# Gate logits with tokens as rows, a route in two parts, and routing masks by comparison, in a perceiver block with mixture of experts

## The chip, the cores and the metric

The kernel runs on one core of a Trainium2 chip. A core has TensorE (matrix products into PSUM banks), VectorE, ScalarE and GpSimd for element-wise work, and SyncE, whose queue issues most DMAs. The engines run their own instruction streams and meet at semaphores. The metric is the device time of one execution in microseconds (us), as the median of three runs. Names in the profile: PE is TensorE, PEld its weight loads, DVE is VectorE, ACT is ScalarE, POOL is GpSimd, SP is SyncE.

## The reference

A block on `x` of 2 batches x 512 tokens x 512 features, with a context of 2 x 8192 x 512. Three residual layers, all in float32:

```python
x = x + cross_attention(layernorm(x), ctx)      # five linear maps, softmax over 8192 keys
x = x + ssm(layernorm(x))                       # state space layer as a long convolution by FFT, gated by silu
x = x + ffn(layernorm(x))                       # mixture of experts

def ffn(x):                                     # 8 experts, one per token
    xt = x.reshape(-1, 512)                     # 1024 tokens
    gates = softmax(xt @ gate_w + gate_b)       # gate_w: 512 x 8
    sel = argmax(gates, axis=-1)                # the first of equal ones
    onehot = one_hot(sel, 8)
    y_all = einsum('td,edh->eth', xt, expert_w) + expert_b[:, None, :]
    return einsum('te,eth->th', onehot, y_all)
```

The change concerns only the last layer: how the expert of each token is found, and how the tokens are gathered for the experts.

## The kernel before

The attention over both batches takes the first 930 us or so. The rest, the tail, is: the gated convolution (spectra, products of spectra on VectorE, back to time, gate), the output projection, then the expert layer. Everything is ordered by hand: each engine has one function `tail()` that calls its steps in the order in which they stand in the queue, and a step waits on semaphores that count finished jobs. `JOBS` lists all results that TensorE leaves in a PSUM bank, in its order; bank numbers follow from the position in that list, modulo 8, and a bank is opened once what stood in it before has been read.

Float32 products at high precision are made in three passes over a high part (rounded, "hi") and a low part (the rest, "lo") of each operand. ScalarE rounds the high parts; the low parts are made by GpSimd or VectorE. `gated_lo` on GpSimd (L2164) makes those of batch 0's gated output, `gated_lo` on VectorE (L1813) those of batch 1, `lo_tiles` (L2020) those of the first four experts' weights W0 to W3, `weight_los` (L1947, VectorE) those of all others.

The expert layer, step by step:
- `turn_ffn` (L974, TensorE): turns the 8 token tiles (128 tokens x 512 features) of the sum `xb`; ScalarE copies each from its bank into `spectra` (`turned_ffn`, L1320). In ScalarE's queue that stands behind `weights(3)`, the rounding of W3, which waits for the load of W3.
- `gate_logits` (L981): products of `gate_raw` (stationary, 128 features x 8 experts) with the turned tokens (moving, 512 or 256 tokens), so that a logit is found at (expert, token). ScalarE copies 8 rows per batch to SBUF (`copy_logits`), and `turn_logits` (L992) turns them by eight small transposes to (token, expert).
- `gate` (L1862, VectorE): completes the layer norm of the logits, finds the largest, and the one-hot `hits`.
- `rank_tokens` (L1001, TensorE): products with the masks `before` (1 where column > partition) and `ones`, which give each token's rank within its expert, and the number of tokens per expert.
- `route` (L1901, VectorE): 15 groups of 128 slots are filled. Groups 0 to 7 hold the first 128 tokens of each expert; a token of rank 128 or more goes to one of 7 spare groups. From rank and counts it finds `lane` (the slot in the group) and `group`, and builds `place` (128x1024, 1 where the token's lane is the column) and `numbered` (token number where the token's group is the column).
- `place_tokens` (L1012, TensorE): 8 products of `place` with `numbered` give, for each slot of each group, the token's number. VectorE makes integer row numbers of them (L1932 for the gather, L1934 for the scatter).
- `gather` (L2199, GpSimd): an indirect DMA fetches the normalized tokens and the sum for the 128 rows of a group from the DRAM tensor `mixed`. It waits also for the stores of both into `mixed` (`store_x`, `store_rows` on SP) and for W3's low parts.
- `turn_tokens` and `mix` (L1020, L1029, TensorE): turn a group's tokens, and 12 products with the group's expert and one with the bias. ScalarE rounds the turned tokens, VectorE makes the low part (`turned_lo`, L1954), then adds the result to the sum (`add_mixed`), and GpSimd scatters the rows to the output.
- `split_expert_bias` (L1891, VectorE): four operations that make high and low parts of the experts' bias, needed by the last product of mix.0.

SP issues in this order (L599 to L620): W0; bias; W1; W2; W4; `store_x(0)`; W3; W5; `store_x(1)`; four `store_rows`; W6; W7; then the seven chosen experts. W3, like W0, goes to the buffer `stage[0]` and waits for W0's low parts as well.

On GpSimd the order is: low parts of the convolution's output; routing numbers (`lanes`, which holds 0 to 127 along a row, among them); the output bias into batch 0's residual; `gated_lo`; `routing_masks` (L2187), which waits until VectorE's products of spectra are done, since it uses their scratch row `obB`; the output bias into batch 1's residual (`add_out_bias(1)`, L2156); W0 to W3.

## Time and profile before

| | us |
|---|---|
| median of 3 runs | 1134.09 |
| lowest, highest | 1133.72, 1135.25 |
| the profiled execution | 1134.54 |
| its span in the trace | 1132.8 |
| busy in the span: TensorE | 1093.9 |
| VectorE | 841.3 |
| ScalarE | 530.5 |
| GpSimd | 537.5 |
| mean granted clock of TensorE | 0.985 of full speed |

TensorE is busy for 97% of the span. Times in the trace are from the span's start. A row of the timeline gives start, duration, engine, line, operation, output and inputs, and how many instructions were merged; the brackets at its end hold the idle time of the engine before the row, and what ended it. The granted clock is 1.00 at full speed (2.4 GHz) and 0.50 at the lower level (1.2 GHz). Matrix products of float32 that aren't split show two passes each, so that four of them are eight instructions in a row of the trace.

### The profile page before, as it was taken

Reading aid. Unit: us, or ns where it says so; the run is one execution under the profiler, and the core shown is the slowest. Engines: PE = TensorE matmul, PEld = TensorE weight load, DVE = VectorE, ACT = ScalarE, POOL = GpSimd, SP = SyncE. Lnnn points to the kernel's source line nnn. Section 1 sums busy time; section 2 is a strip of 40 time slices with the busy share of each in tenths; the row PEclk is TensorE's granted clock in tenths of the full one; section 3 lists DMA queues with packets and bytes.
Section 4 is the critical chain, followed back from the end, with each engine's and each line's share of the span. In section 5 each row is a group of like instructions: output and inputs, shape, how many; then the busy total and the mean of one; then the engine's idle time right before and its main releaser. Section 6 shows DMA issues by size and latency. Waiting matters only on the chain.

```text
span 1132.8 us, 16497 instructions
## 1 busy us (share of the span) xinstructions
PE 1093.9 (97%) x4969; PEld 884.5 (78%) x4969; DVE 841.3 (74%) x1756; ACT 530.5 (47%) x1127; POOL 537.5 (47%) x588
## 2 busy tenths in 40 slices
PE   7999999999999999999999999999999999998498
PEld 5787877878888888888888888888888888886375
DVE  6963498799888888778357777776777657699584
ACT  4221056556555555533464444444444444356462
POOL 3700445345444544411266666665765632177253
PEclk8999999999999999999999999999999999999699
DMA  8211368977876787432429767766876541025991
GB/s 292 84 53 59 52 153 211 218 194 190 204 179 185 190 192 195 140 87 99 76 73 203 193 187 202 187 191 171 213 185 177 179 161 38 1 76 161 323 398 66
DMA packets 199351, 182.26 MB, mean 161 GB/s; under 512 B 17873, under 2 KB 144881, under 8 KB 199299
## 3 DMA queue, kind: packets, MB, share of 16 engines
q1 hardware_dynamic: 178658, 140.21, 48.3%
q10 hardware_dynamic: 17280, 31.46, 7.9%
q0 software_dynamic: 3360, 9.97, 2.4%
q8 instruction: 24, 0.39, 0.1%
q14 instruction: 29, 0.23, 0.1%
HBM read 141.73 MB, written 41.68 MB: 162 GB/s over the span
## 4 chain that ended last, share of the span: by engine, by line
PE 80%; DVE 8%; POOL 4%; DMA 3%; issue 3%; SPq 1%; ACT 1%; POOLq 0%; ACTq 0%; DVEq 0%
PE bank L644 39%; PE bank L783 28%; PE bank L1040 4%; PE bank L837 3%; PE bank L652 1%; PE bank L1026 1%; DMA stage<-in_L_xattn_hW_dram 1%; DVE h L1527 1%; DMA stage<-in_L_ffn_expert_w_dram 1%; DMA spectra<-in_ctx_dram 1%; PE bank L987 1%; PE bank L678 1%; POOL hl_C L2023 1%; PE bank L1045 1%; POOL hl_B L2039 1%
## 5 line engine op out<-in xcount | busy, mean ns | idle before, releaser
L1187 ACT ACTIVATE probs<-bank,nbias 128x512 f32<-128x512 f32 x128 | 88.1, 688 | 242.3 <-DVE nbias L1650 242.1
L783 PE MATMUL bank<-hl_F,probsT 128*128 128x512 f32 x768 | 190.4, 397 | 0.6 <-issue 0.4
L783 PE MATMUL bank<-hl_A,probsT 128*128 128x512 f32 x768 | 190.4, 396 | 0.0
L644 PE MATMUL bank<-hl_B,hl_D 128*128 128x512 f32 x768 | 185.7, 391 | 1.8 <-POOL hl_B L2039 1.4
L1645 DVE TENSOR_REDUCE mx<-bank 128x1 f32<-128x512 f32 x128 | 88.0, 687 | 133.9 <-PE bank L644 133.9
L644 PE MATMUL bank<-hl_C,hl_D 128*128 128x512 f32 x768 | 185.3, 390 | 0.0
L783 PEld LDWEIGHTS bank<-hl_F,probsT 128*128 128x128 f32 x768 | 144.1, 188 | 35.4 <-issue 0.8
L783 PEld LDWEIGHTS bank<-hl_A,probsT 128*128 128x128 f32 x768 | 144.1, 188 | 34.3 <-POOL hl_A L2032 0.2
L644 PEld LDWEIGHTS bank<-hl_B,hl_D 128*128 128x128 f32 x768 | 143.7, 188 | 34.1 <-issue 2.3
L644 PEld LDWEIGHTS bank<-hl_C,hl_D 128*128 128x128 f32 x768 | 144.1, 188 | 31.7 <-issue 0.3
L2032 POOL TENSOR_TENSOR hl_F<-stage,hl_F 128x512 fp32r<-128x512 f32 x64 | 84.7, 1323 | 162.2 <-ACT hl_F L1152 162.1
L2032 POOL TENSOR_TENSOR hl_A<-stage,hl_A 128x512 fp32r<-128x512 f32 x64 | 84.2, 1315 | 145.4 <-ACT hl_A L1152 145.4
L1691 DVE SCALAR_TENSOR_TENSOR rows<-rows,alpha,bank 128x512 f32<-128x512 f32 x128 | 90.9, 710 | 14.9 <-PE bank L783 14.9
L1662 DVE TENSOR_TENSOR probsT<-bank,probsT 128x512 fp32r<-128x512 f32 x128 | 87.3, 682 | 1.9 <-ACT probsT L1174 1.8
L1174 ACT ACTIVATE probsT<-bank 128x512 fp32r<-128x512 f32 x128 | 74.2, 580 | 10.8 <-PE bank L770 10.7
L1152 ACT ACTIVATE hl_F<-stage 128x512 fp32r<-128x512 f32 x64 | 40.4, 632 | 27.7 <-issue 18.2
L1152 ACT ACTIVATE hl_A<-stage 128x512 fp32r<-128x512 f32 x64 | 40.4, 632 | 27.6 <-issue 18.3
L2039 POOL TENSOR_TENSOR hl_C<-spectra,hl_C 128x512 fp32r<-128x512 f32 x32 | 40.9, 1292 | 22.9 <-ACT hl_C L1160 22.9
L2039 POOL TENSOR_TENSOR hl_C<-xb,hl_C 128x512 fp32r<-128x512 f32 x32 | 41.0, 1292 | 20.2 <-ACT hl_C L1160 20.2
L1667 DVE STREAM_TRANSPOSE bank<-resid 128x512 f32<-128x512 f32 x60 | 43.0, 716 | 9.4 <-DMA resid<-p_rows 9.4
L1683 DVE SCALAR_TENSOR_TENSOR lsum<-lsum,alpha,rsum 128x1 f32<-128x1 f32 x128 | 49.0, 383 | 0.0
L1699 DVE SCALAR_TENSOR_TENSOR zT<-h,cbdt,zT 128x512 f32<-128x512 f32 x64 | 46.6, 728 | 0.0
(419 smaller groups left out, 1862.6 us busy)
## 6 DMA issues: line engine op xcount, KB each, us to landing
p_rows<-probs ACTq DMA_DIRECT2D x120, 256.0 KB, 3.1
stage<-in_ctx_dram SPq DMA_DIRECT2D x112, 256.0 KB, 3.2
spectra<-in_ctx_dram SPq DMA_DIRECT2D x64, 256.0 KB, 5.9
xb<-in_ctx_dram SPq DMA_DIRECT2D x64, 256.0 KB, 5.9
resid<-p_rows SPq DMA_DIRECT2D x240, 64.0 KB, 2.1
h<-p_rows SPq DMA_DIRECT2D x120, 64.0 KB, 2.5
obB<-p_rows SPq DMA_DIRECT2D x120, 64.0 KB, 2.0
stage<-in_L_ffn_expert_w_dram SPq DMA_DIRECT2D x6, 1024.0 KB, 6.9
```

The lines of the kernel that those rows point to most:

```text
L644: last = nc.tensor.matmul(dst, lhs[:, a, t, k * P:(k + 1) * P], rhs[:, c, t, :], start=(t == 0 and (a, c) == PASSES[0]), stop=(t == T - 1 ...
L783: last = nc.tensor.matmul(obank[u % 2][:], probsT[u % 2][:, a, j, :], nat[b][par][:, c, j, :], start=(j == 0 and (a, c) == PASSES[0]), sto ...
L1152: nc.scalar.activation(nat[b][par][:, 0, j, :], stage[par][:, j, :], ACT.Copy).then_inc(nat_hi, 1)
L1174: nc.scalar.activation(dst, src, ACT.Copy).then_inc(pT_hi, 1)
L1187: nc.scalar.activation(dst, src, ACT.Exp, bias=nbias[:, q:q + 1], scale=SCALE, accum_out=rsum[:, q:q + 1]).then_inc(probs_ready, 1)
L1645: nc.vector.tensor_reduce(mx[:, col], sbank[u % 2][:], AX_X, ALU.max).then_inc(stat_done, 1)
L1662: nc.vector.tensor_tensor(lo, src, hi, ALU.subtract).then_inc(pT_split, 1)
L1683: nc.vector.scalar_tensor_tensor(lsum[:, col], lsum[:, col], alpha[:, u:u + 1], rsum[:, col], ALU.mult, ALU.add).then_inc(sums_updated, 1)
L1691: nc.vector.scalar_tensor_tensor(rows[:, q, :], rows[:, q, :], alpha[:, u:u + 1], obank[u % 2][:], ALU.mult, ALU.add).then_inc(rows_added, 1)
L1699: nc.vector.scalar_tensor_tensor(kern[:, k, :], h[u % 2][:], weight, kern[:, k, :], ALU.mult, ALU.add).then_inc(term_added, 1)
L2032: nc.gpsimd.tensor_tensor(nat[b][par][:, 1, j, :], stage[par][:, j, :], nat[b][par][:, 0, j, :].bitcast(F32), ALU.subtract).then_inc(nat_s ...
L2039: nc.gpsimd.tensor_tensor(by_squares(ctxT[par][:, 1])[:, dd], square(squares[b][par], dd), by_squares(ctxT[par][:, 0])[:, dd].bitcast(F32) ...
```

## The change

Six edits:
1. Logits by tokens. `gate_logits(n)` now takes the turned tile as the stationary operand and `gate_raw` as the moving one: four products of 128x128 with 128x8 per tile, which leave the logits at (token, expert) in the bank `logit_columns` at once. The jobs `logits@0`, `logits@1`, `copy_logits` and `turn_logits` go. The products of a tile follow two turned tiles behind.
2. Route in two parts. Groups 0 to 7 need only the rank and the token's own expert, so a first `place` is built from `rank`, and `slots.0` gives gather and scatter rows for them. The rest of the route follows, and a second `place` from `lane` and `slots.1` for the spare groups.
3. The second turn of tokens is put into mix.0, behind its first three products.
4. Masks by comparison: `ones` is `lanes` x 0 + 1, `before` is `lanes` > `partition`; no scratch, so no wait for the products. They stand before `gated_lo`.
5. W0's low parts stand right behind `gated_lo`, now with the wait for the products in front of them, and `add_out_bias(1)` behind them.
6. `split_expert_bias` stands behind the route instead of before `gate`.

```diff
@@ JOBS @@
-             + tiles_at(0, "x_ssm")[2:] + tiles_at(1, "x_ssm") + tiles_at(0, "ffnT") + tiles_at(1, "ffnT")[:2]
-             + ["logits@0"] + tiles_at(1, "ffnT")[2:] + ["logits@1", "logit_columns", "ranks", "slots"] + MIX_JOBS)
+             + tiles_at(0, "x_ssm")[2:] + tiles_at(1, "x_ssm") + tiles_at(0, "ffnT") + tiles_at(1, "ffnT")
+             + ["logit_columns", "ranks"] + (["slots.0", "slots.1"]) + MIX_JOBS)
@@ TensorE @@
-                for t in range(T):
-                    turn_ffn(0, t)
-                for t in range(2):
-                    turn_ffn(1, t)
-                gate_logits(0, 1)
-                for t in range(2, T):
-                    turn_ffn(1, t)
-                gate_logits(1, 2)
-                turn_logits()
+                for n in range(B * T + 2):
+                    if n < B * T:
+                        turn_ffn(n // T, n % T)
+                    if n >= 2:
+                        gate_logits(n - 2)
                 rank_tokens()
-                place_tokens()
+                place_tokens("slots.0", 1, 0, E)
+                place_tokens("slots.1", 2, E, E)
                 turn_tokens(0)
                 for g in range(GROUPS):
-                    if g + 1 < GROUPS:
+                    if 0 < g < GROUPS - 1:
                         turn_tokens(g + 1)
                     mix(g)
...
+            def gate_logits(n):
+
+                dst = bank_of("logit_columns")
+                if n == 0:
+                    open_bank("logit_columns")
+                evacuated_from(f"ffnT.{n % T}@{n // T}")
+                for k in range(T):
+                    last = nc.tensor.matmul(dst[:, n * E:(n + 1) * E], spectra[:, n, k * P:(k + 1) * P], gate_raw[:, k, :],
+                                            start=(k == 0), stop=(k == T - 1))
+                if n == B * T - 1:
+                    last.then_inc(filled, 1)
...
+            def place_tokens(job, count, first, width):
+
+                pe.wait_ge(ranked, count)
+                dst = open_bank(job)
                 for n in range(B * T):
-                    last = nc.tensor.matmul(dst[:, 0:2 * E], place[:, n, :], numbered[:, n, :], start=(n == 0), stop=(n == B * T - 1))
+                    last = nc.tensor.matmul(dst[:, 0:width], place[:, n, :], numbered[:, n, first:first + width],
+                                            start=(n == 0), stop=(n == B * T - 1))
...
@@ mix, in the loop over t @@
+                    if g == 0 and t == 0:
+                        turn_tokens(1)
@@ ScalarE @@
                 turned_ffn(0, range(T))
-                turned_ffn(1, range(2))
-                copy_logits(0)
-                turned_ffn(1, range(2, T))
-                copy_logits(1)
+                turned_ffn(1, range(T))
@@ VectorE, gate @@
                 dve.wait_ge(iota_made, 1)
+                nc.vector.tensor_tensor(numbered[:, :, 0:E], hits.bitcast(F32), of_token(token), ALU.mult)
@@ VectorE, route @@
-                nc.vector.tensor_reduce(rank, hit_value, AX_X, ALU.add)
+                link(nc.vector.tensor_reduce(rank, hit_value, AX_X, ALU.add))
+                place_at(rank)
...
+                filled_by(dve, "slots.0")
+                nc.vector.tensor_scalar(gather_rows[:, 0:E], bank_of("slots.0")[:, 0:E], float(FAR), float(TOKENS - 1),
+                                        ALU.add, ALU.min).then_inc(indexed, 1)
...
+                place_at(lane)
+                choose_experts()
+                filled_by(dve, "slots.1")
+                nc.vector.tensor_scalar(gather_rows[:, E:GROUPS], bank_of("slots.1")[:, 0:SPARE], float(FAR), float(TOKENS - 1),
+                                        ALU.add, ALU.min).then_inc(indexed, 1)
...
+            def place_at(m):
+
+                nc.vector.tensor_tensor(place, m.unsqueeze(2).to_broadcast([P, B * T, P]),
                                         lanes.unsqueeze(1).to_broadcast([P, B * T, P]), ALU.is_equal).then_inc(ranked, 1)
@@ VectorE, tail @@
                 scale_outputs()
-                split_expert_bias()
                 gate()
                 route()
+                split_expert_bias()
@@ GpSimd, routing_masks @@
-                pool.wait_ge(product_step, PRODUCTS * (TRIPS + 2))
-                whole = obB[:, 2 * P:3 * P]
-                chain(nc.gpsimd.memset(whole, 1.0))
-                nc.gpsimd.tensor_copy(ones, whole).then_inc(table_made, 1)
-                pool.wait_ge(table_made, 1)
-                chain(nc.gpsimd.affine_select(out=whole, in_=whole, compare_op=ALU.is_gt, fill=0.0, base=0,
-                                              pattern=[[1, P]], channel_multiplier=-1))
-                nc.gpsimd.tensor_copy(before, whole).then_inc(table_made, 1)
+                pool.wait_ge(iota_made, 1)
+                nc.gpsimd.tensor_scalar(ones, lanes, 0.0, 1.0, ALU.mult, ALU.add).then_inc(table_made, 1)
+                nc.gpsimd.tensor_scalar(before, lanes, partition, None, ALU.is_gt).then_inc(table_made, 1)
@@ GpSimd, tail @@
                 add_out_bias(0)
+                routing_masks()
                 gated_lo()
-                routing_masks()
+                pool.wait_ge(product_step, PRODUCTS * (TRIPS + 2))
+                lo_tiles("W0", raw[BUF["W0"]], weights_hl[0])
                 add_out_bias(1)
-                for g in range(EARLY):
+                for g in range(1, EARLY):
                     lo_tiles(f"W{g}", raw[BUF[f"W{g}"]], weights_hl[g])
...
                 for g in range(ROWS_KEPT):
                     gather(g)
+                pool.wait_ge(indexed, 2)
```

The order of instructions on TensorE around the logits, before: `ident,xb` are the turns of a tile, `spectra,gate_raw` the logits, `ident,probs` the first of the small transposes.

```order
L978 MATMUL bank<-ident,xb 128x128 [waits evacuated]
L978 MATMUL bank<-ident,xb 128x128 x3
L987 MATMUL bank<-spectra,gate_raw 8x512 [waits copied,evacuated]
L987 MATMUL bank<-spectra,gate_raw 8x512 x3
L978 MATMUL bank<-ident,xb 128x128 [waits evacuated]
L978 MATMUL bank<-ident,xb 128x128 x3
```

And after the change, where the pattern repeats for every tile:

```order
L974 MATMUL bank<-ident,xb 128x128 [waits evacuated]
L974 MATMUL bank<-ident,xb 128x128 x3
L984 MATMUL bank<-gate_raw,spectra 128x8 [waits copied]
L984 MATMUL bank<-gate_raw,spectra 128x8 x3
L974 MATMUL bank<-ident,xb 128x128 [waits evacuated]
L974 MATMUL bank<-ident,xb 128x128 x3
L984 MATMUL bank<-gate_raw,spectra 128x8 [waits copied]
```

The wide products, four for a batch, became four narrow ones for each tile; each group of four waits for the copy of its own tile alone.

VectorE from the rank on, after the change: `place` is written by L1927 (twice), the gather rows by L1901 and L1921, the bias split is L1880 to L1883, and L1951 is the low part of the first turned tokens.

```order
L1927 TENSOR_TENSOR dft<-ssm_in,ssm_w 128x1024 [waits link_done]
L1896 TENSOR_TENSOR ssm_in<-ssm_in,ssm_w 128x56
L1898 TENSOR_REDUCE ssm_in<-ssm_in 128x8 [waits link_done]
L1899 SCALAR_TENSOR_TENSOR ssm_in<-ssm_w,ssm_in 128x8 [waits link_done]
L1901 TENSOR_SCALAR gather_rows<-bank 128x8 [waits filled,link_done]
...
L1921 TENSOR_SCALAR gather_rows<-bank 128x7 [waits filled]
L1923 TENSOR_SCALAR scatter_rows<-bank 128x7
L1880 CAST dft<-probs 16x512 [waits iota_made,in_eb]
L1881 TENSOR_TENSOR h<-probs,dft 16x512 [waits link_done]
L1882 SCALAR_TENSOR_TENSOR probs<-h,ssm_w 16x512 [waits link_done]
L1883 SCALAR_TENSOR_TENSOR dft<-dft,ssm_w,probs 16x512 [waits link_done]
L1951 TENSOR_TENSOR probsT<-bank,probsT 128x512 [waits rounded]
```

Before, these four operations of the bias stood ahead of `gate`, there was one `place` (L1928) near the end of the route, and L1957, the low part of the first turned tokens, followed the scatter rows directly.

GpSimd in the tail, before: L2192 to L2197 are the masks, `zT<-zT,h` the output bias into batch 1's residual, `hl_C<-stage` W0's low parts, `hl_F<-zT` the gated low parts.

```order
L2167 TENSOR_TENSOR hl_F<-zT,hl_F 128x512 [waits gated_hi0] x4
L2192 MEMSET obB 128x128 [waits product_step,filled]
L2193 CAST dft<-obB 128x128 [waits table_step]
L2195 AFFINE_SELECT obB<-obB 128x128 [waits table_made]
L2197 CAST dft<-obB 128x128 [waits table_step]
L2162 TENSOR_TENSOR zT<-zT,h 128x512 [waits resid_scaled,in_outb]
L2162 TENSOR_TENSOR zT<-zT,h 128x512 [waits resid_scaled] x3
L2023 TENSOR_TENSOR hl_C<-stage,hl_C 128x512 [waits split_hi] x4
```

And after:

```order
L2185 TENSOR_SCALAR dft<-ssm_w 128x128 [waits iota_made,filled]
L2186 TENSOR_SCALAR dft<-ssm_w 128x128
L2161 TENSOR_TENSOR hl_F<-zT,hl_F 128x512 [waits gated_hi0] x4
L2017 TENSOR_TENSOR hl_C<-stage,hl_C 128x512 [waits split_hi,product_step]
L2017 TENSOR_TENSOR hl_C<-stage,hl_C 128x512 [waits split_hi] x3
L2156 TENSOR_TENSOR zT<-zT,h 128x512 [waits resid_scaled,in_outb]
L2156 TENSOR_TENSOR zT<-zT,h 128x512 [waits resid_scaled] x3
```

The masks moved ahead of the gated low parts, and W0's low parts ahead of the bias into batch 1's residual.

## Rows read from the trace of the kernel before

**Rows 1.** Timeline of TensorE: start and duration in us, then the row

```profile
1034.63 2.78 PE L978 MATMUL bank<-ident,xb 128*128 128x128 f32 x24
1040.23 3.59 PE L987 MATMUL bank<-spectra,gate_raw 128*8 128x512 f32 x8 [2.82 <-ACT spectra L1224]
...
1051.67 0.30 PE L1007 MATMUL bank<-onehot,dft 128*128 128x64 f32 x1 [2.19 <-DVE onehot L1885]
...
1058.46 1.88 PE L1017 MATMUL bank<-dft 128*128 128x16 f32 x8 [4.86 <-DVE dft L1928]
1066.20 1.09 PE L1026 MATMUL bank<-ident,spectra 128*128 128x128 f32 x4 [5.86 <-DMA spectra<-mixed,gather_rows]
1068.95 1.09 PE L1026 MATMUL bank<-ident,spectra 128*128 128x128 f32 x4 [1.67 <-DMA spectra<-mixed,gather_rows]
1069.69 4.28 PE L1040 MATMUL bank<-hl_C,probsT 128*128 128x512 f32 x12
...
1074.74 3.06 PE L1040 MATMUL bank<-hl_B,probsT 128*128 128x512 f32 x12
```

**Rows 2.** Timeline of ScalarE, same columns

```profile
1035.95 2.19 ACT L1341 ACTIVATE hl_F<-stage 128x512 fp32r<-128x512 f32 x4 [3.54 <-DMA stage<-in_L_ffn_expert_w_dram]
1038.05 3.00 ACT L1224 ACTIVATE spectra<-bank 128x512 f32<-128x512 f32 x6
...
1048.93 2.91 ACT L1330 ACTIVATE rows<-xb,ffn_shift,rstd 128x512 f32<-128x512 f32 x4
```

**Rows 3.** Timeline of SyncE's queue, same columns

```profile
1027.72 0.37 SPq L554 DMA_DIRECT2D mixed<-xb  x1
1028.13 0.51 SPq L437 DMA_DIRECT2D stage<-in_L_ffn_expert_w_dram  x1
```

**Rows 4.** Timeline of GpSimd, same columns

```profile
994.20 11.85 POOL L2167 TENSOR_TENSOR hl_F<-zT,hl_F 128x512 fp32r<-128x512 f32 x4 [27.39 <-ACT hl_F L1288]
...
1010.00 2.16 POOL L2193 CAST dft<-obB 128x128 fp32r<-128x128 f32 x1
...
1017.85 6.85 POOL L2023 TENSOR_TENSOR hl_C<-stage,hl_C 128x512 fp32r<-128x512 f32 x4
```

**Rows 5.** Timeline of VectorE, same columns

```profile
1001.54 1.67 DVE L376 TENSOR_TENSOR spectra<-probs,obB 128x512 f32<-128x512 f32 x1
...
1043.76 0.41 DVE L1895 CAST dft<-probs 16x512 fp32r<-16x512 f32 x1
...
1045.69 0.74 DVE L1898 SCALAR_TENSOR_TENSOR dft<-dft,ssm_w,probs 16x512 fp32r<-16x512 f32 x1
...
1049.59 0.23 DVE L1876 TENSOR_TENSOR logit<-bank,ssm_in 128x64 f32<-128x64 f32 x1 [3.02 <-PE bank L998]
...
1054.10 0.22 DVE L1909 TENSOR_REDUCE ssm_in<-ssm_in 128x8 f32<-128x64 f32 x1
...
1054.72 0.22 DVE L1913 TENSOR_TENSOR ssm_in<-ssm_in,ssm_w 128x56 f32<-128x56 f32 x1
...
1057.19 1.22 DVE L1928 TENSOR_TENSOR dft<-ssm_in,ssm_w 128x1024 fp32r<-128x1024 f32 x1
...
1060.37 0.17 DVE L1932 TENSOR_SCALAR gather_rows<-bank 128x15 int32<-128x15 f32 x1 [1.06 <-PE bank L1017]
...
1067.95 0.69 DVE L1957 TENSOR_TENSOR probsT<-bank,probsT 128x512 fp32r<-128x512 f32 x1 [7.32 <-ACT probsT L1347]
1068.56 2.49 DVE L1951 TENSOR_TENSOR hl_E<-stage,hl_E 128x512 fp32r<-128x512 f32 x4
```

**Rows 6.** Line L897: duration min/median/max in ns, first and last start

```profile
L897 PE MATMUL bank<-gate_raw,one x8: 256/256/276, 938.8 to 939.6; 128*128 128x8 f32 x8
```

**Rows 7.** Gathers into `qc`, line L2202, same columns

```profile
L2202 POOL DMA_INDIRECT qc<-mixed,gather_rows x3: 933/1382/1414, 1069.2 to 1107.0; - x3
```

**Rows 8.** Two stretches: length, TensorE's busy time, clock, DMA share, GB/s

```profile
932.00:940.00 8.00, 7.94 (x58) 1.00 0.26 101
1066.00:1073.00 7.00, 5.14 (x17) 0.54 0.98 335
```

53 lines of the change are left out of this document (12 added, 41 removed).

## Prediction

> **What bounds the kernel now.** I read the slices, then the chain of waits over the last 100 us, then each engine's timeline from 990 us. The attention stages are bound by TensorE and the change doesn't touch them. It touches the stretch from about 994 us to the first expert product (mix.0) at 1069. Behind that, TensorE runs 15 experts back to back, so the last instruction moves as mix.0 moves. The question is therefore: when do the first turned tokens and mix.0 start?
>
> In that stretch TensorE waits six times [rows 1]: 2.82 us for copied turned tiles (until 1040.23), then for the logits to come through a copy, 2.19 us for the one-hot, 4.86 us for VectorE's route (until 1058.46), 5.86 us for the first gather (until 1066.20), 1.67 us for the second (until 1068.95). Three orders stand behind these waits:
> - ScalarE copies turned tiles only after W3's split, which waits 3.54 us for W3 to land and ends at 1038.1 [rows 2]. SP issues W3 at 1028.13, right behind the store of batch 0 at 1027.72 [rows 3]. It is a queue behind VectorE's last sum of batch 0. The chain of waits blames GpSimd's splits, but W0's split ended at 1017.85 + 6.85 = 1024.7 [rows 4], 3.4 us before.
> - VectorE works on the route from 1053.7 to 1058.4 [rows 5], TensorE then forms the slots in 1.88 us [rows 1], and gather rows follow at 1060.37.
> - mix.0 stands behind the second gather on TensorE.
>
> **Logits by tokens.** Removed: the wide products (3.59 us, and as much again for batch 1), two copies of 8 rows and eight small transposes behind them. Added: 8 tiles x 4 products, stationary 128x128, moving 8 columns. The same form stands in L897: its 8 passes (two per product) start between 938.8 and 939.6, so one each 0.115 us [rows 6]. A tile costs 4 x 2 x 0.115 = 0.92 us, eight cost 7.3 us. Their advantage is the start: the first needs one copied tile, not four. Copies run at 3.00 / 6 = 0.5 us spacing from 1038.05, the first is done at 1038.65 [rows 2], and TensorE starts about 1038.8. Only three of eight tiles are turned by then, five remain at 2.78 / 6 = 0.46 us [rows 1]. End: 1038.8 + 7.3 + 5 x 0.46 + about 0.1 = 1048.5 to 1048.7. VectorE got its logits at 1049.59. The gain is 0.9 us; bounds 0 (each tile pays its fill of 0.1 to 0.15) and 1.6 (switching between tiles hides some loads, start at once).
>
> ScalarE loses the two copies and so normalizes earlier than 1048.93, by about 2.5 us; row stores and the loads of W6 and W7 go earlier with it. Hidden, but needed: the gather waits for those stores. They now stand ready at about 1056, the gather rows at 1056.8: 0.7 us of cover. Uncovered it costs up to 1 us.
>
> **Route in two parts.** Before: hits x ranks, rank (L1909, 1054.10 + 0.22), 15 small operations, and place until 1057.19 + 1.22 = 1058.41 [rows 5]. Now place (1.22) stands right behind rank: 1054.35 to 1055.57. TensorE's slots.0 takes 1.88 again (its loads set it, not 8 or 16 columns): 1057.50. The gather rows of the eight fixed experts are at 1057.5 instead of 1060.37, 2.9 us earlier. The three small operations between hide under TensorE. But the second part begins only then: from L1913 to the end of place it was 1058.41 - 1054.72 = 3.69 us, which gives about 1061.3. TensorE has slots.1 in its queue ahead of the first turned tokens, so it is busy with that until 1061.3 + 1.9 = 1063.2. The first gather, at its old distance 1066.20 - 1060.37 = 5.83, lands at 1063.3: the two meet, and slots.1 costs nothing so far.
>
> **The bias split behind the route.** It was hidden in VectorE's wait for logits: 1043.76 to 1045.69 + 0.74 = 1046.43, 2.67 us [rows 5]. Now it follows scatter rows.1 and stands ahead of the turned tokens' low part: 1063.4 to 1066.0. The turned tokens would be ready for it at 1063.3 + 1.75 = 1065.0 (1067.95 - 1066.20 before), so it costs 1.0 us. The low part (0.69) ends at 1066.7 and mix.0 starts at about 1066.75.
>
> **Mixing one before the second turn.** Before, TensorE's unbroken work began with the second turn at 1068.95. Now it begins with mix.0's first three products, and the second turn sits inside; the work is the same. So the gain counts from 1068.95 to 1066.75: 2.2 us. With the 0.9 of the logits: 3.1 us. Bounds of this part: 1.2 (gather 1 us later, because more of W6 and W7 is in flight) to 3.2 (the bias split hidden entirely).
>
> **Masks and W0 on GpSimd.** The masks lose a memset, a select and their wait. They move from 1010 into the 27.39 us in which GpSimd was idle before 994.20 [rows 4]; ScalarE's order (spectra copied before the gated tiles that release 994.20) puts them there. Two tensor_scalar of 128x128 are new; the nearest row, a cast of that size, took 2.16 us while VectorE worked on two SBUF inputs, and one of 512 columns free of that costs about a quarter of 5 us. So 0.3 us each on their own. But they fall in VectorE's product stretch. There GpSimd's four low parts took 11.85 us, and a VectorE operation of 0.6 took 1.67 us [rows 4, 5]. Each mask can hold VectorE once for its own length, or wait itself and push the low parts. VectorE is what leads to the store at 1027.72, to W3 and the logits, one for one. Bounds 0 and 1.5 us (two masks, each holding a product and the low parts behind them); I take 0.6.
> W0's split now runs from 1010 on, and the out bias follows. SP issues W3 behind the store anyway, so this brings nothing; the out bias is needed after 1027 and ends by 1024. Which of GpSimd's tiles meets VectorE's gated low parts changes: plus or minus 0.5, taken as 0. The scatters' wait for indexed 2 (1063.4) is over long before mix.0 ends.
>
> **A rule against it.** VectorE's second part and the bias split now run beside GpSimd's gathers; before, GpSimd stood idle during the route. The rows that show such a pair: hl_E's low parts took 2.49 us for four, undisturbed [rows 5], and the gathers into qc, of which the first started beside them, took 0.93 us at least and 1.41 at most [rows 7], so GpSimd gave way. The linked small operations leave gaps, and there it could be the other way. I take 0.2 us.
> The Trainium skill, "SBUF — State Buffer" (section on the two sides and the shared port pair), says that VectorE with two SBUF inputs and GpSimd hold the pair exclusively, the loser waiting a whole instruction. By that rule a gather could stop the linked chain again and again. The trace agrees for GpSimd's tensor_tensor (1.67 instead of 0.6 us) and, for gathers, only in that they lengthen.
>
> **Sum.** 0.9 + 2.2 - 0.6 - 0.2 = 2.3 us. The profiled run took 1134.54 us (span 1132.8 and 1.7 around it), 0.45 above the median 1134.09; 2.3 off each gives 1132.2 and 1131.8. The forecast is 1131.8.
>
> **Rivals.**
> 1. The clock returns earlier (chance 0.12). It was low as mix.0 began: 1066 to 1073 has a mean of 0.54 [rows 8], which is 0.50 until about 1072.4 and 1.00 from there. Now slots.1 and the first turn stand against each other, and work goes on sooner, so mix.0 could run at full clock: 3.06 instead of 4.28 us [rows 1], and the turn at half its 1.09: up to 1.6 us more, 1130.2. Against it: it took 3.4 us of unbroken work from 1068.95, and the turn at 1066.20 had not raised it.
> 2. The gain is eaten upstream (0.24): masks cost 1.5 in place of 0.6, or the row stores become the gather's last wait (1 us), or logits bring nothing. Gain about 1.0: 1133.1.
> 3. Slower, by the ports (0.07). Gathers stop VectorE in the second part and the bias split. Two or three gathers fall in the former and two in the latter, at 0.93 us each: up to 4.65 us, of which 0.2 is counted. The change loses from the third such stop on; at five it is 4.45 - 2.3 = 2.15 us later than before: 1136.2. For it: linked operations leave gaps. Against: the gathers gave way where both ran.
> 4. Slower, by the clock (0.05). TensorE now does only turns and 8-column products from 1034.6 to 1048.6. If it falls to the low level around 1042, the remaining 6.6 us double: 1138.4. Against it: from 932 to 940 TensorE did turns and L897's products only and stayed at 1.00 [rows 8].
> 5. Nothing moves (0.02): something else orders the first gather.
>
> **Numbers.** The forecast has 0.50. About 0.2% (2.27 us) is what can be told from no change. The forecast lies on that edge. Half of its cases and all of rival 1 and a little of rival 2 count as faster: 0.52; slower by more 0.08; the rest 0.40. The forecast's own range is 1130.8 to 1132.8; with rivals 1 and 2 and the bounds above, 1129.9 to 1134.2, which leaves out rivals 3 and 4 and a little at the low end.
>
> **What would show it.** Right: the first 8-column product near 1038.8 to 1039.5, logits taken at 1048.7, gather rows about 3.7 us earlier than 1060.37, slots.1 ending as the first gather lands, the bias split right ahead of the first low part, mix.0 near 1066 (all plus what the masks cost). Wrong: a second product tile spacing above 1.0 us; a clock below 1.00 before 1049; small VectorE operations of 1 us in the second part; GpSimd's first gather released by a store and not by the gather rows; W3 issued apart from the store of batch 0.

## The result, and the profile after

| | before | after |
|---|---|---|
| median of 20 runs, us | 1135.66 | 1139.28 |
| lowest, highest | 1133.15, 1138.63 | 1135.82, 1143.66 |
| profiled run and its span | 1134.54, 1132.8 | 1137.05, 1135.0 |

The ratio is 1.0031, 95% interval 1.0022 to 1.0041: the change makes the kernel 3.5 us slower, where 2.3 us faster was forecast. The sign is wrong, and the time lies outside the range.

The changed kernel's TensorE timeline (start and duration in us, then the row; a bracket is the idle time ahead and what ended it), for [rows 1]:

```profile
1035.64 1.47 PE L974 MATMUL bank<-ident,xb 128*128 128x128 f32 x12
1038.15 1.03 PE L984 MATMUL bank<-gate_raw,spectra 128*128 128x8 f32 x8 [1.03 <-ACT spectra L1215]
1039.03 0.64 PE L974 MATMUL bank<-ident,xb 128*128 128x128 f32 x4
1039.50 0.96 PE L984 MATMUL bank<-gate_raw,spectra 128*128 128x8 f32 x8
1040.32 0.63 PE L974 MATMUL bank<-ident,xb 128*128 128x128 f32 x4
1040.79 1.67 PE L984 MATMUL bank<-gate_raw,spectra 128*128 128x8 f32 x8
...
1048.10 5.13 PE L984 MATMUL bank<-gate_raw,spectra 128*128 128x8 f32 x24
1055.42 0.42 PE L995 MATMUL bank<-onehot,dft 128*128 128x64 f32 x1 [2.19 <-DVE onehot L1869]
...
1059.58 1.87 PE L1005 MATMUL bank<-dft 128*128 128x8 f32 x8 [2.03 <-DVE dft L1927]
1065.34 1.87 PE L1005 MATMUL bank<-dft 128*128 128x8 f32 x8 [3.89 <-DVE dft L1927]
1067.32 1.09 PE L1015 MATMUL bank<-ident,spectra 128*128 128x128 f32 x4
1070.82 1.62 PE L1029 MATMUL bank<-hl_C,probsT 128*128 128x512 f32 x3 [2.41 <-DVE probsT L1951]
...
1072.94 3.26 PE L1029 MATMUL bank<-hl_C,probsT 128*128 128x512 f32 x9
```

The first two tiles of gate products take 1.03 and 0.96 us, the third 1.67, and all others 1.71 or 1.72 (the last row is three of them in 5.13). The turns go from 0.64 to 1.09. The granted clock goes with it; stretches of TensorE with length, then the busy time of TensorE, of its weight loads, VectorE, ScalarE and GpSimd, then clock, DMA share and GB/s. The first and the last row answer [rows 8]:

```profile
932.00:940.00 8.00, 8.00 (x48) 6.17 (x46) 5.91 (x10) 5.48 (x12) 6.85 (x16) 1.00 0.01 2
1034.00:1040.00 6.00, 4.97 (x38) 4.40 (x37) 5.69 (x14) 3.94 (x8) 3.96 (x4) 1.00 0.10 37
1040.00:1046.00 6.00, 6.00 (x36) 6.00 (x35) 2.99 (x13) 1.60 (x4) 1.00 (x1) 0.57 0.49 139
1046.00:1052.00 6.00, 6.00 (x30) 6.00 (x30) 0.00 (x0) 4.14 (x7) 0.00 (x0) 0.50 0.69 258
...
1066.00:1073.00 7.00, 4.48 (x18) 3.65 (x18) 6.05 (x14) 0.60 (x1) 5.48 (x6) 0.50 0.91 293
```

The clock falls from 2.4 to 1.2 GHz at about 1041 and stays there, though TensorE is busy for all of 1040 to 1052. It is at 0.50 in mix.0 as well: its last nine products take 3.26 us.

The other engines. ScalarE, SyncE's queue, GpSimd and VectorE, for [rows 2 to 5]:

```profile
1035.33 2.19 ACT L1328 ACTIVATE hl_F<-stage 128x512 fp32r<-128x512 f32 x4 [3.42 <-DMA stage<-in_L_ffn_expert_w_dram]
1037.43 1.55 ACT L1215 ACTIVATE spectra<-bank 128x512 f32<-128x512 f32 x3
...
1048.84 2.91 ACT L1317 ACTIVATE rows<-xb,ffn_shift,rstd 128x512 f32<-128x512 f32 x4
```

```profile
1027.22 0.37 SPq L553 DMA_DIRECT2D mixed<-xb  x1
...
1053.19 1.77 SPq L559 DMA_DIRECT2D mixed<-zT  x2
```

```profile
1006.31 6.71 POOL L2017 TENSOR_TENSOR hl_C<-stage,hl_C 128x512 fp32r<-128x512 f32 x4 [3.64 <-DVE spectra L375]
...
1062.66 1.24 POOL L2191 DMA_INDIRECT spectra<-mixed,gather_rows  x1 [21.66 <-DVE gather_rows L1901]
```

```profile
1006.15 2.38 DVE L1794 TENSOR_TENSOR hl_D<-spectra,hl_D 128x512 fp32r<-128x512 f32 x2
1008.46 3.42 DVE L1794 TENSOR_TENSOR hl_B<-spectra,hl_B 128x512 fp32r<-128x512 f32 x2
...
1053.34 0.23 DVE L1860 TENSOR_TENSOR logit<-bank,ssm_in 128x64 f32<-128x64 f32 x1 [9.97 <-PE bank L984]
...
1061.56 0.17 DVE L1901 TENSOR_SCALAR gather_rows<-bank 128x8 int32<-128x8 f32 x1 [1.45 <-PE bank L1005]
...
1067.25 0.17 DVE L1921 TENSOR_SCALAR gather_rows<-bank 128x7 int32<-128x7 f32 x1 [0.81 <-PE bank L1005]
1067.40 0.41 DVE L1880 CAST dft<-probs 16x512 fp32r<-16x512 f32 x1
...
1070.00 0.67 DVE L1951 TENSOR_TENSOR probsT<-bank,probsT 128x512 fp32r<-128x512 f32 x1
```

VectorE gets its logits at 1053.34, not at 1048.7. It waited 9.97 us for them. The gather is released by the gather rows, as forecast. ScalarE starts to normalize at 1048.84, 0.1 us earlier than before and not 2.5: it copies the turned tiles first, and they came late too. VectorE's low parts of batch 1's convolution output (L1794, L1810 before) were 1.28 us for two before; they took 2.38 and 3.42 beside GpSimd's W0, which now starts in the same stretch.

The lines that answer to [rows 6, 7], with durations (min/median/max) in ns and first and last start:

```profile
L896 PE MATMUL bank<-gate_raw,one x8: 256/256/276, 935.3 to 936.1; 128*128 128x8 f32 x8
```

```profile
L2191 POOL DMA_INDIRECT qc<-mixed,gather_rows x3: 938/1152/2152, 1071.7 to 1110.7; - x3
```

To compare executions, I cut each timeline at four places: the first turn of `turn_ffn`; the first product released by the one-hot; the first product of mix.1; the end of the span. Each number is a difference of starts in that kernel's TensorE timeline.

| us | first turn at | to one-hot | to mix.1 | to end | span |
|---|---|---|---|---|---|
| before | 1034.63 | 17.04 | 23.07 | 58.06 | 1132.8 |
| after | 1035.64 | 19.78 | 21.55 | 58.03 | 1135.0 |
| after, second execution (e12) | 1034.98 | 24.22 | 22.43 | 58.07 | 1139.7 |

So the loss is in the logits (2.7 and 7.2 us), the route gives back 1.5 and 0.6, and behind mix.1 nothing has changed. The two executions differ in the logits because in e12 the first gate product starts 4.61 us behind the first turn (2.51 in the first), and its first tile already takes 1.74 us: the clock went down as it began. The row of before is one of the better executions of that kernel as well: in e2, e4, e7 and e8, whose logits are as before, the one-hot comes 18.70 to 19.28 us behind the first turn and not 17.04 (why is shown under e9).

### The profile page after: what moved, and what is told of

The parts are those of the page before. It is cut to its first block, busy times and chain, and to the rows that moved or that the text cites. A ratio compares the mean times of both kernels' runs of the same rounds, so it can differ in the third digit from the quotient of the medians.

```text
span 1135.0 us, 16577 instructions
## 1 busy us (share of the span) xinstructions
PE 1100.4 (97%) x5009; PEld 896.1 (79%) x5009; DVE 844.2 (74%) x1760; ACT 530.3 (47%) x1125; POOL 538.9 (47%) x586
## 3 DMA queue, kind: packets, MB, share of 16 engines
q0 software_dynamic: 3360, 9.97, 2.5%
## 4 chain that ended last, share of the span: by engine, by line
PE 83%; DVE 11%; DMA 2%; issue 1%; SPq 1%; ACT 1%; POOL 1%; POOLq 0%; ACTq 0%; DVEq 0%
PE bank L643 40%; PE bank L782 30%; PE bank L1029 4%; PE bank L836 2%; PE bank L651 1%; PE bank L984 1%; DVE probs L375 1%; PE bank L1015 1%; DVE h L1511 1%; DMA stage<-in_L_ffn_expert_w_dram 1%; DMA spectra<-in_ctx_dram 1%; DVE spectra L375 1%; PE bank L1036 1%; PE bank L677 1%; DVE bnst L1489 0%
```

## The experiments

**Which edit loses the time.** Three kernels, each the kernel before with one edit or one group.

`e3_logits_alone`: before with edit 1 alone.

```diff
...
-    gate_logits(0, 1)
...
-    gate_logits(1, 2)
-    turn_logits()
+    for n in range(B * T + 2):
+        if n < B * T: turn_ffn(n // T, n % T)
+        if n >= 2: gate_logits(n - 2)
...
```

> The kernel before with the logits by tokens alone. Theory B: the clock falls to 0.50 within the logits, they are ready about 3.5 to 4.5 us later than before, and the kernel is that much slower. Rival C: no gap ahead of it, so the clock stays at 1.00, the logits are ready 0.9 us earlier and the kernel is 0.9 us faster.

Measured: 1139.75 us against 1134.2, ratio 1.0044 (1.0030 to 1.0058), +5.0 us. In its TensorE timeline one-hot comes 22.66 us after the first turn, 5.6 later than before, and mix.1 follows 23.12 after that, as before.

```profile
1039.02 1.03 PE L983 MATMUL bank<-gate_raw,spectra 128*128 128x8 f32 x8 [2.83 <-ACT spectra L1211]
1039.91 0.64 PE L973 MATMUL bank<-ident,xb 128*128 128x128 f32 x4
1040.38 1.58 PE L983 MATMUL bank<-gate_raw,spectra 128*128 128x8 f32 x8
...
1050.06 5.13 PE L983 MATMUL bank<-gate_raw,spectra 128*128 128x8 f32 x24
```

By themselves the narrow logits cost as much as the whole change or more (+3.4 to +6.6 us against +2.5 to +4.7, by the intervals). The first half of the expectation came true, with 5.0 us where 3.5 to 4.5 were expected.

`e2_gpsimd_alone`: before with edits 4 and 5 (masks by comparison and early, W0 behind the gated lows).

```diff
-    gated_lo()
-    routing_masks()
+    routing_masks()
+    gated_lo()
+    pool.wait_ge(product_step, PRODUCTS * (TRIPS + 2))
+    lo_tiles("W0", raw[BUF["W0"]], weights_hl[0])
...
```

> The kernel before with the GpSimd edits alone (masks by comparison and early, W0's low parts right behind the gated ones). Theory A: VectorE's four low parts take 5 to 6 us, TensorE waits about 3.5 us for them, the kernel is 2.5 to 3 us slower than before. Rival D: the early masks cost it, in VectorE's product stretch; then VectorE's products there are over 1 us longer and the four low parts as before.

Measured: 1134.51 us, ratio 0.9997 (0.9984 to 1.0010). GpSimd's new order can't be told from no change (-1.8 to +1.1 us). VectorE's L1810 takes 1.28 us twice there, so neither of the two cases that were expected came true.

`e4_route_alone`: before with edits 2, 3 and 6.

```diff
-    place_tokens()
+    place_tokens("slots.0", 1, 0, E)
+    place_tokens("slots.1", 2, E, E)
...
-    split_expert_bias(); gate(); route()
+    gate(); route(); split_expert_bias()
...
```

> The kernel before with the route in two parts, the bias split behind it and the second turn inside mix.0. Both theories: the part of the forecast that held, 1.9 to 2.2 us faster than before; slots.1 and the bias split lie between the first gather and mix.0. Rival E (ports in the route): small VectorE operations beside the gathers stretch, and it is under 1 us faster.

Measured: 1135.48 us, ratio 1.0011 (0.9996 to 1.0026): no gain, where 1.9 to 2.2 us were expected. One-hot to mix.1 is 23.69 us, against 23.07 before. Its GpSimd and TensorE timelines:

```profile
1057.61 1.25 POOL L2216 DMA_INDIRECT spectra<-mixed,gather_rows  x1 [18.99 <-DMA mixed<-zT]
```

```profile
1065.26 1.09 PE L1028 MATMUL bank<-ident,spectra 128*128 128x128 f32 x4 [4.02 <-DMA spectra<-mixed,gather_rows]
```

Its gather rows are written at 1055.59, but the gather starts only at 1057.61, 2.02 us later where it is 1.10 before (1060.37 to 1061.47), and what releases it is a row store. It then needs 7.65 us until TensorE can turn its rows; before it was 1066.20 - 1061.47 = 4.73 (turn from [rows 1], gather from this row of before):

```profile
1061.47 1.25 POOL L2202 DMA_INDIRECT spectra<-mixed,gather_rows  x1 [19.87 <-DVE gather_rows L1932]
```

**Is GpSimd's W0 part of the loss?** VectorE's slow low parts (L1794) in the first profile suggested so.

`e1_w0_behind_lows`: after, with GpSimd's W0 low parts held until those of VectorE (L1794) are done.

```diff
-    pool.wait_ge(product_step, PRODUCTS * (TRIPS + 2))
+    pool.wait_ge(y_lo_done[1], 2 * T)
```

> The changed kernel, but GpSimd starts W0's low parts only when VectorE's four last low parts of batch 1's output are done, not when the products are. Theory A (ports): W0's low parts stretched those four from 2.5 to 5.8 us and made TensorE wait 3.46 us; here they take 2.5 us again, TensorE waits less than 0.6 us there, and the kernel is 2.8 us faster than the changed one, at +0.8 us against before. Theory B (clock): the products of 8 columns let the clock fall in the logits by themselves; it falls here too, near the third tile. Rival C: the clock fell in the logits only as a late effect of that 3.46 us gap; then it stays at 1.00 here, and the kernel is 6 to 7 us faster than the changed one, 3 us faster than before.

Measured: 1138.9 us, ratio 1.0046 (1.0028 to 1.0065). L1794 is 1.28 twice there, and the time is no better than after's. The first theory, that this was most of the loss, failed, and so did rival C: the clock falls in the logits without that stop of TensorE. Theory B came true; here the fall is within the second tile.

`e12_after_again`: the changed kernel once more.

> The changed kernel again, to see in a second execution what varies from run to run. Expected: 1139 us, granted clock 0.981 over the span, the gate products at 1.71 us each from 1041 on. Of the stop of VectorE in the evacuation of the lows (L1794: 2.38 and 3.42 us in the first profile, 1.28 twice in the kernels without it) one theory says it belongs to the changed order and comes back with the same durations; the other says it is a race between GpSimd's product and VectorE's evacuation that is lost only in some executions: 1.28 twice here, with no change of the median.

Measured: 1138.89 us, ratio 1.0037 (1.0023 to 1.0051). VectorE's timeline of the unchanged order:

```profile
1009.60 1.28 DVE L1794 TENSOR_TENSOR hl_D<-spectra,hl_D 128x512 fp32r<-128x512 f32 x2
1010.81 1.28 DVE L1794 TENSOR_TENSOR hl_B<-spectra,hl_B 128x512 fp32r<-128x512 f32 x2
```

GpSimd's W0 begins at 1009.76 there, behind VectorE's 1009.60. In the first profile it was 1006.31 behind 1006.15: the same 0.16 us, and another outcome. So it varies from execution to execution: of the five profiles with W0 in this place, two show 2.38 and 3.42 or near it (after and e14) and three 1.28 twice (e2, e12, e13). The first profile lost 4.5 us there (TensorE waited 3.46 us for `hl_B`, then three of its groups behind ran at the low clock). How often it happens isn't known; e1, in which it can't, has the same median as e12. In its span it hardly shows, because that execution was early: the products of [rows 6] started at 938.8 before and at 935.3 after, 3.5 us ahead in code that the change doesn't touch, and the first turn 1.0 us behind.

**Why the clock falls.** In e1, e3 and e12 it falls within 1.5 us of the end of a gap of 2.65 to 3.13 us, so their traces can't separate two theories (in after the gap is 1.03 us, and the clock falls 2.7 us behind it): there are no wide products in the stage any more (they would hold or restore the clock); or it is the gap of TensorE ahead of the stage that lowers it.

`e5_logits_one_wide` and `e6_logits_three_wide`: e3 with one, or three, unused products of 448 columns ahead of each tile's gate products.

```diff
     evacuated_from(f"ffnT.{n % T}@{n // T}")
+    for _ in range(1):    # 3 in e6
+        nc.tensor.matmul(dst[:, 64:512], probsT_all[:, 0, 0, 0, :], inverse[...], start=True, stop=True)
     for k in range(T):
```

> The kernel before with logits by tokens, and one extra product of 448 columns (0.19 us, result unused, into columns of the same bank that nothing reads) ahead of each tile's four. Theory B (clock, because the stage has no wide products): the clock stays at 1.00 through the logits or comes back within them; the four products of a tile take about 1.0 us, the logits are ready 1 to 3 us earlier than with logits by tokens alone, although 1.5 us of work is added. Rival F (the clock falls there whatever TensorE does, or one wide product per tile is too little): as with logits by tokens alone or 1.5 to 3 us slower than that.

> The same with three extra wide products per tile (0.57 us each tile, 4.5 us in all at full clock). Theory B: clock 1.00 from the third tile on at the latest, each tile's own products 1.0 us, logits ready at about the same time as with logits by tokens alone (4.5 us more work, 4.5 us less by the clock). Rival F: the clock stays at 0.50, and the logits come 4.5 to 9 us later than with logits by tokens alone.

Measured: 1145.16 us, ratio 1.0077 (1.0050 to 1.0104), and 1152.37 us, ratio 1.0150 (1.0120 to 1.0180). Both are slower than expected (one-hot 4.9 and 11.4 us later behind the first turn than in e3; at most 3 and 9 were expected). TensorE stood 3.37 and 3.97 us ahead of the first extra product, and the clock was at 0.50 from that product on (0.71 us for it in e5), every gate tile took 1.71, and it never returned. One to three wide products among the narrow ones don't bring the clock back. Whether they could have held it isn't tested, since it was down before they began.

`e9_fill_before_logits`: before (wide logits) with 11 unused products of 512 columns in TensorE's gap ahead of the first logits product.

```diff
     dst = open_bank(f"logits@{b}")
+    if b == 0:
+        filler(dst, 11)    # matmul(dst, probsT_all[...], inverse[...][:, 0:512])
...
```

> The kernel before with nothing changed but 11 products of 512 columns, whose result nobody reads, put into TensorE's gap of some 2.8 us between its last work of stage one and the first logits product (a bf16 pass of that width at full clock is about 0.21 us, so they just fill the gap). Theory A: what drops the granted clock at the logits is the idle stretch just ahead of them; then the first eight wide logits products (L987 there) take 3.6 us and not the 5.28 us that four of my earlier profiles with wide logits show, the window over the logits reads 1.00, and the kernel is about 1.7 us faster than before's median run. Rival B: the fall is due to the turns and the light work over the last 10 us, and the fillers move nothing: 5.28 us again, ratio 1.000. Rival C: the fillers run at half clock themselves and push the logits back by up to 2 us: 1.5 us slower.

Measured: 1133.52 us against 1135.18, ratio 0.9984 (0.9972 to 0.9997), -1.8 us. The first of the two rows is e2's, the second e9's; both are the first eight wide products:

```profile
1040.49 5.28 PE L987 MATMUL bank<-spectra,gate_raw 128*8 128x512 f32 x8 [2.79 <-ACT spectra L1224]
```

```profile
1038.36 3.60 PE L996 MATMUL bank<-spectra,gate_raw 128*8 128x512 f32 x8 [0.33 <-ACT spectra L1233]
```

The kernel before loses its clock at the logits too, in some executions. Of six profiles with wide logits and the gap, four show 5.28 or 5.29 us (e2, e4, e7, e8) and two 3.59 (before and e13); all four with the gap filled show 3.60. But with wide products it comes back inside the stage. e2's stretches:

```profile
1040.00:1046.00 6.00, 5.51 (x11) 1.14 (x12) 5.48 (x17) 1.52 (x4) 1.87 (x2) 0.72 0.36 106
1046.00:1052.00 6.00, 5.09 (x32) 2.55 (x30) 1.26 (x4) 3.10 (x6) 0.00 (x0) 1.00 0.68 243
```

`e10_narrow_with_fill`: e3 with 10 such products ahead of the first gate product.

```diff
     if n == 0:
         open_bank("logit_columns")
+        filler(dst, 10)
```

> The kernel before with the logits by tokens alone (as e3_logits_alone), and 10 unused products of 512 columns ahead of the first gate product. If the idle stretch ahead is all that drops the clock, the narrow gate products and the turns run at 1.00 to the end of the logits (a gate product of 8 passes-pairs 1.03 us each, not 1.71) and the time is that of before or up to 1 us less. If the narrow stage cannot hold the clock by itself, it falls some 3 to 5 us later than in e3_logits_alone (where it fell at 1040.4), most products still show 1.71 us, and the time is 2 to 4 us above before. I lean to the second: 0.65 against 0.35.

Measured: 1140.40 us, ratio 1.0063 (1.0037 to 1.0089). Its timeline and stretches:

```profile
1037.41 4.10 PE L965 MATMUL bank<-probsT 128*128 128x512 f32 x10 [3.14 <-ACT spectra L1219]
1041.31 1.03 PE L991 MATMUL bank<-gate_raw,spectra 128*128 128x8 f32 x8
...
1044.77 1.00 PE L980 MATMUL bank<-ident,xb 128*128 128x128 f32 x4
1045.56 1.72 PE L991 MATMUL bank<-gate_raw,spectra 128*128 128x8 f32 x8
```

```profile
1041.00:1045.00 4.00, 4.00 (x36) 3.90 (x35) 3.66 (x13) 1.19 (x2) 0.00 (x0) 0.93 0.65 186
1045.00:1052.00 7.00, 7.00 (x36) 7.00 (x35) 0.14 (x2) 2.48 (x5) 0.00 (x0) 0.50 0.52 193
```

The fillers missed their gap: the bank opens only with ScalarE's copy, so they stand behind the 3.14 us and not in them. The clock fell as they began (it is at 0.53 over 1038 to 1039), they ran mostly at 0.50 (4.10 us for ten), and it came back at about 1041.5. That makes this the cleaner test: the gate products and turns begin at full clock, TensorE has no idle time from 1037.41 on, and from about 1045 the clock is at 0.50 again and stays through the stage. The narrow stage doesn't hold the clock by itself. That is the second case of the expectation, but it was priced at 2 to 4 us above before and cost 7.2 (4.2 to 10.1).

**Where the gain of the route goes.** The rivals were the row stores and the loads of W6 and W7 beside the gather.

`e7_route_late_loads` is e4, and `e8_late_loads_alone` is before, with W6 and W7 issued after the second gather has landed.

```diff
+    sp.wait_ge(gathered[1], 16)
     fixed_load(6)
     fixed_load(7)
```

> The kernel before with the route in two parts, the bias split behind it, the second turn inside mix.0, and SP issuing W6 and W7 only when the second gather has landed. Theory G: in the route alone the gather rows came early, but the first gather landed 7.6 us after its issue instead of 4.7, since row stores and W6, W7 were still in flight. Here it lands in 4.0 to 4.7 us, slots.1 and the bias split become the last waits, and the kernel is 2 us faster than before. Rival H: the gather is slow for another reason (GpSimd's descriptors beside VectorE's route); then it still takes over 6 us.

> The kernel before with W6 and W7 issued only when the second gather has landed, nothing else. Theory G: the first gather lands about 1 to 1.5 us sooner after its issue than in the kernel before (4.7 us), so up to 1.5 us faster; if later expert loads come late in turn, no change. The route's own gain is the difference to the run with both.

Measured: 1136.3 us, ratio 1.0011 (0.9996 to 1.0027), and 1138.65 us, ratio 1.0021 (1.0007 to 1.0034). e7's timelines:

```profile
1059.35 1.25 POOL L2217 DMA_INDIRECT spectra<-mixed,gather_rows  x1 [18.46 <-DMA mixed<-zT]
```

```profile
1064.07 1.09 PE L1029 MATMUL bank<-ident,spectra 128*128 128x128 f32 x4 [0.55 <-DMA spectra<-mixed,gather_rows]
```

The gather lands 4.72 us after its start instead of 7.65, and one-hot to mix.1 is 20.63 us, 2.4 less than before: the size that was forecast. But from mix.1 to the end both late-load kernels take 59.8 and 59.98 us instead of 58.06. What is won at the first gather is paid back behind it, when the weights come late: ScalarE waits up to 3.3 us in e7 and 2.6 in e8 for a weight load behind mix.1, and never in before. So the kernel isn't 2 us faster as expected.

e8 also bounds what W6 and W7 do. Its first gather starts at the old place, with the two loads held back:

```profile
1061.87 1.25 POOL L2203 DMA_INDIRECT spectra<-mixed,gather_rows  x1 [20.82 <-DVE gather_rows L1933]
```

TensorE can turn its rows at 1066.63, 4.76 us later, where 1 to 1.5 us less than before's 4.73 was expected. So the loads don't slow the gather of before. They were issued at 1055.14 there, 6.3 us ahead of it. The profiles with W6 and W7 ahead of the gather fall into two groups by that distance: with W6 issued 3.7 to 5.0 us ahead of the first gather, it takes 7.09 to 7.65 us to the turn (e4, e13, and e11, e14, e15 below); with 6.1 us or more, 4.67 to 5.00 (before, e2, e3, e5, e6, e9, e10). In after, e1 and e12 the turn stands behind slots.1 and doesn't show it. The row stores don't make this difference: in e7 the gather starts 5.1 us behind the issue of the first zT store and takes 4.72, in e4 5.6 us behind it and takes 7.65.

**Taking the logits back.** `e13_after_wide_logits`: after, with edit 1 undone and all else kept.

```diff
-    for n in range(B * T + 2):
...
+    gate_logits(0, 1)
...
+    gate_logits(1, 2)
+    turn_logits()
...
```

> The changed kernel with only the logits put back to the wide form (one product over four tiles, then turns), everything else as changed. If the narrow logits are the whole loss, this is 1134.5 to 1136, ratio to before 0.999 to 1.001: the +5.0 us of the logits gone, and the route's two parts giving 0 to 0.5 us, as in e4_route_alone, because the row stores and the loads of W6 and W7 hold the first gather. If the loss had another part in the combination (GpSimd's new order with the later bias split), it stays at 1137 or more.

Measured: 1136.80 us against 1135.48, ratio 1.0014 (0.9998 to 1.0029), just above what was expected (1134.5 to 1136, ratio up to 1.001). Undoing the logits takes back 2 us or so of the 3.5 to 4, and what stays cannot be told from no change. Its one-hot to mix.1 is 23.25 us: with the logits early, the route's two parts give nothing, as in e4. So the edits don't simply add. With the logits late they do: +5.0 (e3) and -0.6 to -1.5 (route in after, from the table) make +3.5 to +4.4, where +3.5 and +4.2 (0.0037 of 1135.18) were measured. The intervals of the single terms are as wide as the differences between them, so this sum supports the reading and doesn't prove it.

**A version that beats both.** `e11_fill_all_gaps` is e9 with unused products also ahead of the ranks (8), the slots (20), the first turn (24) and the second (6). `e15_fill_longer_turn` has 34 instead of 24. `e14_after_wide_filled` is e13 with such fillers.

```diff
...
+    filler(open_bank("ranks"), 8)
     rank_tokens()
+    filler(open_bank("slots"), 20)
     place_tokens()
+    filler(open_bank("turned.0"), 24, True)    # 34 in e15
     turn_tokens(0)
+    filler(open_bank("turned.1"), 6, True)
```

> The kernel before with unused products in every gap of TensorE around the route: 11 ahead of the logits, 8 ahead of the ranks, 20 ahead of the slots, 24 ahead of the first batch's turn and 6 ahead of the second's. Theory: all small stages from the logits to the first mix run at half clock in before because TensorE stands in between; with the gaps filled the ranks, the slots and mix.0 run at full clock, which gives 1.7 us at the logits, about 1 us at ranks and slots and 1 to 2 us in mix.0: 3 to 4 us faster than before (1132). Rival: the fillers delay the work behind them by as much (each gap ends at another engine's result, and a filler that starts late ends late): 0 to 2 us slower.

> e11_fill_all_gaps with 34 instead of 24 unused products ahead of the first batch's turn: there the gap after them was 2.81 us and the clock fell once more (0.73 over 1064 to 1070), so that the second turn took 1.06 us and the first mix 3.62 us instead of about 0.64 and 3.05. If the clock holds, 0.6 to 1.0 us less than e11_fill_all_gaps; if the gather lands earlier than in that profile, the fillers overshoot and cost up to 1 us.

> e13_after_wide_logits with unused products in TensorE's gaps: 11 ahead of the logits, 8 ahead of the ranks, 8 and 17 ahead of the two slot products, 16 ahead of the first batch's turn, 6 ahead of the first mix. Clock theory: 1.00 through to the gather, so the logits are 1.7 us earlier, ranks and both slot products take half (0.8 us each earlier), and the first mix runs at 1.00: 3 to 4 us less than e13 and 0.997 of before, as e11_fill_all_gaps, or 1 us better. If the first gather is held by the row stores in the DMA queues as in e4_route_alone, the earlier indices buy nothing more and the time is that of e11_fill_all_gaps within 1 us.

| | median, us | ratio | clock over the span |
|---|---|---|---|
| e11 | 1132.86 | 0.9974 (0.9957 to 0.9991) | 0.994 |
| e15 | 1132.39 | 0.9978 (0.9965 to 0.9990) | 0.998 |
| e14 | 1134.42 | 0.9992 (0.9977 to 1.0006) | 0.995 |

e15's TensorE timeline around mix.0, now at full clock throughout:

```profile
1057.29 8.00 PE L974 MATMUL bank<-dft 128*128 128x512 f32 x34
1065.99 0.63 PE L1039 MATMUL bank<-ident,spectra 128*128 128x128 f32 x4 [0.71 <-DMA spectra<-mixed,gather_rows]
...
1068.20 3.04 PE L1053 MATMUL bank<-hl_C,probsT 128*128 128x512 f32 x12
```

mix.0's twelve products take 3.04 us instead of 4.28 [rows 1], and one-hot to mix.1 21.70 instead of 23.07. More was to be had: the gather rows come 1.5 us sooner behind the one-hot than before, but the first gather then takes 7.32 us to the turn and not 4.73. e11 and e15 are 3 and 2.5 us faster than before; each other's, and e9's, intervals overlap, so neither the ten further products of e15 nor the four further places of both are shown to add to e9's 1.8 us in the median. e14 is the weaker one and can't be told from before (22.94 us to mix.1). Its fillers end 2.57 us before the first gather lands, and the clock is at 0.50 again from about 1068 to 1071. Its gather starts 4.1 us behind its gather rows (1061.26 against 1057.16), released by a row store, and takes 7.09 us. So the indices of the two-part route are early there too, and of no use.

## Why the prediction was wrong

**Logits by tokens: +0.9 forecast, -5.0 measured.** This is the step that failed. The durations were right (a tile and its turn take 1.35 and 1.29 us at full clock, 0.92 + 0.46 = 1.38 forecast), the start nearly (1038.15 in place of 1038.8), and the sum assumed the full clock throughout. At 0.50 a tile takes 1.71 and a turn 1.09, 2.45 us from one tile's start to the next. It is rival 4, with its place (around 1042) nearly right, and its net price nearly (1138.4 against 1134.09, so +4.3; +3.5 measured), and it was given 0.05. That the price came so near is in part luck: in the profiles of e1, e3 and e12 the clock fell between 1039.8 and 1040.6, and the stage took 22.6 to 24.2 us to the one-hot in place of after's 19.78. What spoke against it was a wrong analogy: 932 to 940 kept 1.00 in [rows 8], but in those 8 us only the last one or so is narrow products, eight passes from 938.8 on [rows 6], and from 939.74 products of 512 columns follow; the rest is turns of 128 columns. The logits have 64 such passes. One window with a similar list of operations was taken for evidence on a stage with other shares.

**The route in two parts: +2.2 forecast; 1.5 and 0.6 measured in after, 1.1 in e1, nothing in e4 and e13.** In the first profile the steps came out nearly as written: the gather rows were 6.14 us behind the one-hot (1061.56 - 1055.42; 1057.5 - 1051.67 = 5.8 forecast), the first gather had landed when slots.1 ended (the turn starts 0.11 us behind it), the bias split delayed the first low part by 0.9 (1070.00 against 1067.32 + 1.75; 1.0 forecast). By the forecast's own measure, from the one-hot to the second turn before (17.28) and to mix.0 after (15.40), the gain is 1.88 us, 1.88 again in e12 and 1.89 in e1, where 2.2 were forecast. Part of it is lost in mix.0, whose work was counted as the same: its products took 1.62 + 3.26 = 4.88 us instead of 4.28 (5.27 in e1, 5.76 in e12). But this holds only with late logits, when the row stores are out. Where the logits are wide (e4, e13, e7), the gather starts 1.5 to 2.0 us behind its rows, since it waits for a store, and not 1.1; this is in rival 2, there priced at 1 us. And with W6 issued 3.7 us ahead of it, the gather takes 2.9 us longer (e4); the bounds had 1 us for that, and this is the larger part. The 0.7 us of cover that the forecast counted is not tested: it rests on ScalarE normalizing 2.5 us earlier without its two copies, which e4, e7 and e13 still have, and with the low clock of after it normalized only 0.1 us earlier.

**Masks and W0 on GpSimd: -0.6 forecast, 0 measured** (e2: 0.9997, whose interval doesn't exclude 0.6 us). VectorE's low parts (L1810) begin at 1009.53 in e2's profile as in before's, and the products of [rows 6] at 938.6 and 938.8, so the masks held up at most 0.2 us there. In after the masks took 0.30 and 1.57 us between 982.17 and 984.03 on GpSimd. W0 was expected to meet VectorE's gated low parts, at plus or minus 0.5. It met those of the convolution's output instead, and cost 4.5 us in the first profile and nothing in three others (e2, e12 and e13). The Trainium skill, "SBUF — State Buffer" (section on who interferes with whom), says that the engine that issues first keeps the shared port pair for its whole instruction. The trace agrees in that one of the two engines is held: 3.42 us for two of VectorE's operations that take 1.28 otherwise, and, where VectorE is not held, 7.24 us for GpSimd's four (e12) that take 5.06 by themselves (e1). Which one it is can't be read from the starts of the two groups, 0.16 us apart in both cases.

**Gathers against VectorE: -0.2 forecast.** Nothing of it can be seen on the path: VectorE's second part runs from 1061.72 to 1065.29 in after, 3.57 us where 3.69 were counted, and the bias split takes its 2.67 us again. It was the gathers that gave way: the second, beside it, took 1.92 us (0.94 before).

**The clock in mix.0 (rival 1, 0.12)** didn't return earlier. In the six profiles with the two-part route and no fillers mix.0's products took 4.88 to 5.76 us (after, e1, e4, e7, e12, e13), in the eight others without fillers around the route 4.15 to 5.21. A reason that fits, but that no run isolates: before, the second turn ran at the low clock just ahead of them, and now they are the first unbroken work themselves.

**The chances.** That of a clearly faster kernel, 0.52, doesn't follow from its terms: half of 0.50, all of 0.12 and a little of 0.24 make about 0.4.

What stays open: whether the route's two parts have a cost of their own with wide logits (e4, e13 and e7 all lie 1.2 to 1.6 us above before by their ratios, each interval touching zero), whether the clock would hold in a narrow stage with wide products in it from its start, and why the clock falls ahead of the wide logits in some executions only.

## What to carry to other kernels

A stage's time at full clock is not its time: before TensorE's work is cut into narrow products, price it at both clock levels, and look for a stretch of the trace that has the same shares of narrow and wide work for as long, not just the same kinds. If TensorE stands in short gaps ahead of small stages on the critical path, unused products in those gaps are a cheap trial (here 1.8 us for one place, 2.5 and 3 us for five, with intervals that overlap), but check that the filler can start when the gap starts. An index that is ready earlier is worth only what the stores and the DMA engines that its gather needs let it be.
